# An edge stage of gathers and masked sums against one of dense products over counted edges, in a graph-attention and expert kernel on one core

## The reference, cut to what matters

```
x: 2500 nodes x 512;  src, dst: 40000 edges, sorted by dst
x = x + gnn(layernorm(x));   x = x + ffn(layernorm(x))

def gnn(nodes):
    h = nodes @ W + b_w                          # 2500 x 512
    s_dst, s_src = h @ a[:512], h @ a[512:]
    e = leaky_relu(s_dst[dst] + s_src[src] + b_a, 0.2)
    w = exp(e)
    alpha = w / segment_sum(w, dst)[dst]
    return segment_sum(alpha[:, None] * h[src], dst)

def ffn(x):   # 8 experts 512 -> 256 -> 512, the best 2 of a node, weighted by the softmax
```

## Time and profile before

| what | us |
|---|---|
| median of 3 runs (770.01, 776.66, 770.19) | 770.19 |
| the profiled execution, from its first to its last instruction | 843.5 |
| of that, up to the first gather | 85.5 |
| from there to the reciprocal of the denominators | 486.2 |
| from there to the end | 271.8 |

### The profile page before, as it was taken

One profiled execution on the slowest core, in us unless ns is written; L12 is line 12 of the kernel. 1 busy time (PEld: TensorE's weight loads), 2 busy tenths in 40 slices (PEclk: granted clock), 3 DMA queues, 4 the chain that ended last, 5 costly groups with the idle time before them and its releaser, 6 DMA issues.

```text
span 843.5 us, 13398 instructions
## 1 busy us (share of the span) xinstructions
PE 630.6 (75%) x2874; PEld 497.9 (59%) x2875; DVE 456.8 (54%) x1139; ACT 356.8 (42%) x956; POOL 478.4 (57%) x550
## 2 busy tenths in 40 slices
PE   4997335766676757766686667774988899999992
PEld 2886224655564646655565555662645787888881
DVE  3999224564555546645555655579758433333331
ACT  3232323343443434433443434335864444545551
POOL 4461775666665666656666566501104377777773
PEclk9999677989999998798979889995998999999997
DMA  9482675656666656666666666505897277777765
GB/s 310 154 286 103 179 211 146 194 166 178 186 177 174 187 168 189 175 183 167 185 184 182 169 179 189 164 2 188 306 352 285 66 136 133 137 135 134 138 117 71
DMA packets 59260, 147.26 MB, mean 175 GB/s; under 512 B 8965, under 2 KB 18437, under 8 KB 58968
## 3 DMA queue, kind: packets, MB, share of 16 engines
q0 software_dynamic: 35216, 106.84, 50.3%
q1 hardware_dynamic: 24008, 40.01, 13.7%
HBM read 118.46 MB, written 28.35 MB: 174 GB/s over the span
## 4 chain that ended last, share of the span: by engine, by line
PE 45%; DVE 21%; issue 14%; DVEq 7%; another core or an unknown queue 6%; DMA 3%; SPq 1%; ACT 1%; POOLq 0%; POOL 0%; ACTq 0%
PE ps L686 22%; PE ps L825 8%; PE ps L839 6%; DVE acc L1171 4%; DVE S L1162 4%; DVE Wt L1150 3%; DVE junk L1096 3%; PE ps L736 2%; PE ps L815 2%; DVE rows L1089 1%; DMA x_all<-in_x_dram 1%; DVEq L1202 1%; DVEq L1171 1%; PE ps L727 1%
## 5 line engine op out<-in xcount | busy, mean ns | idle before, releaser
L686 PE MATMUL ps<-rows,S 128*128 128x257 f32 x1252 | 325.9, 423 | 156.9 <-DVE acc L1171 107.1
L508 POOL DMA_INDIRECT rows<-node_table,srcT x313 | 298.4, 953 | 178.5 <-issue 86.7
L686 PEld LDWEIGHTS ps<-rows,S 128*128 128x128 f32 x1252 | 263.1, 214 | 219.5 <-issue 160.7
L915 ACT ACTIVATE E<-sdst_w,rows 128x128 f32 x313 | 100.1, 390 | 284.0 <-DVE Wt L1150 187.7
L1171 DVE TENSOR_TENSOR acc<-acc,ps 64x514 f32 x160 | 110.1, 688 | 147.8 <-PE ps L686 68.6
L1162 DVE SCALAR_TENSOR_TENSOR S<-ps,lane,Wt 128x128 f32<-128x128 f32 x313 | 88.2, 345 | 26.3 <-issue 13.9
L915 ACT ACTIVATE ps<-sdst_w,rows 128x128 f32 x313 | 96.0, 350 | 0.0
L825 PE MATMUL ps<-W_e,xgT 128*128 x352 | 83.4, 380 | 0.0
L604 POOL DMA_INDIRECT out_dram<-y,si x44 | 70.4, 1601 | 12.1 <-issue 6.3
L825 PEld LDWEIGHTS ps<-W_e,xgT 128*128 128x128 f32 x352 | 63.4, 190 | 6.9
L645 PE MATMUL ps<-Wb,xT 128*128 128x512 f32 x240 | 56.5, 398 | 6.0 <-DVE Wb L1108 5.0
(11 more groups left out here) (202 smaller groups left out, 612.9 us busy)
## 6 DMA issues: line engine op xcount, KB each, us to landing
W_e<-in_L_ffn_W_dram SPq DMA_DIRECT2D x16, 512.0 KB, 8.9
node_table<-rows SPq DMA_DIRECT2D x20, 258.0 KB, 3.2
xf<-in_x_cols_dram SPq DMA_DIRECT2D x10, 512.0 KB, 6.1
out_dram<-acc SPq DMA_DIRECT2D x20, 256.0 KB, 2.6
xn_table<-xn SPq DMA_DIRECT2D x20, 256.0 KB, 2.4
rows<-node_table,srcT POOLq DMA_INDIRECT x313
x_all<-in_x_dram SPq DMA_DIRECT2D x19, 256.0 KB, 6.6
b_b<-in_L_ffn_b_dram SPq DMA_DIRECT2D x1, 2048.0 KB, 14.6
```

Of the source, the lines that this page charges most:

```text
L508: nc.gpsimd.indirect_dma_start(out=rows[:, g % RING, c, :], out_offset=None, in_=table, in_offset=bass.IndirectOffsetOnAxis(ap=srcT[:, GC ...
L686: m = pe.matmul(ps_agg[q][:, a, 0:HALF], S[:, w, c, :], rows[:, r, c, a * HALF:(a + 1) * HALF], start=(c == 0), stop=(c == n - 1))
L915: m = nc.scalar.activation(e[:, c, :], sdst_w[:, bass.ds(w, 1), :].rearrange("p w n -> p (w n)"), ACT.Exp, bias=bias, scale=scale)
```

## The change: what it does

The edge stage is replaced; the node stage is altered, and the expert stage loses the sum of x and acc/denominator.

The nodes are laid out anew, 125 to a tile. h is kept in SBUF as an fp32r part `H_hi` (a copy by ACT from `hrow`) and a rest `H_lo` (a subtraction by POOL); `node_table`, its stores, the gathers and the ring go. An edge is the pair (lo, key): lo is src modulo 125, key is dst * 20 + src // 125. A tile of 125 targets has 2500 keys, five PSUM banks of 500, ten halves of 250. For each half three chunks of 128 edges are compared (with these inputs no half needs a fourth, so the branches for extras are not taken): DVE writes two bf16 one-hots for a chunk, 250 and 128 wide (`hot`), 60 instructions a tile, and PE multiplies them, 30 matmuls of 250 columns, so that a bank holds the counts. ACT makes the dense weights of a tile, exp(relu(0.8 s) + 0.2 s), with 40 instructions of 125 columns for two tiles ahead (`weights_of`). DVE multiplies weights and counts bank by bank, reading the bank in the order k, n where it is stored n, k (`weigh`), sums them over k (`sums_and_low`), and forms the rest `A_lo` beside ACT's fp32r copy `A_hi`. PE then forms 60 products of 512 columns a tile: A_lo H_hi, A_hi H_hi, A_hi H_lo. The counts of the next tile stand behind every fourth of the first 20 products and every fourth of the next 20; the last 20 have none. `add_x` divides and adds x.

```diff
+            def tile_products(t, s):                                  # PE
...
+                for k in range(NT):
+                    if k % (NT // 4) == 0:
+                        pe.wait_ge(A_lo_ok, 4 * t + k // (NT // 4) + 1)
+                    m = pe.matmul(ps_agg[s][0:TN, :], A_lo[:, k, :], H_hi[:, k, :], start=(k == 0), stop=False)
...
+                    if k % 4 == 3 and counts:
+                        count(t + 1, k // 4)
+                for k in range(NT):
+                    for H in (H_hi, H_lo.bitcast(F32R)):
+                        m = pe.matmul(ps_agg[s][0:TN, :], A_hi[:, s, k, :], H[:, k, :], start=False,
...
+                    if k < NT // 2 and k % 2 == 1 and counts:
+                        count(t + 1, NT // 4 + k // 2)
+                    if k == NT // 2 - 1 and counts:
+                        count_extras(t + 1)
...
+            def hot(key, low, chunk, half):                           # DVE
+
+                nc.vector.tensor_scalar(key, lane_k[:, :], offset[:, bass.ds(half, 1)],
+                                        keyT[:, bass.ds(chunk, 1)], ALU.add, ALU.is_equal)
+                return nc.vector.tensor_scalar(low, lane_l[:, :], loT[:, bass.ds(chunk, 1)], None,
+                                               ALU.is_equal)
+
+            def pairs_of(t):
+
+                words_of(dve, regs, t)
+                for h in range(HALVES):
+                    first_chunk = dve.snap(within(dve.snap(regs[h]), 0, CH - 1))
+                    if not (isinstance(t, int) and t == 0 and h < SLOTS):
+                        dve.wait_ge(count_ok, HALVES * t + h + 1 - SLOTS)
+                    for c in range(BASE - h % 2):
+                        m = hot(hot_k[:, h % SLOTS, c, :], hot_l[:, h % SLOTS, c, :], first_chunk + c, t * HALVES + h)
...
+            def weigh(t, s):
+
+                dve.wait_ge(exp_ok, t + 1)
+                for b in range(BANKS):
+                    dve.wait_ge(bank_ok, BANKS * t + b + 1)
+                    part = weight[:, s, :, b * BN:(b + 1) * BN]
+                    nc.vector.scalar_tensor_tensor(out=part, in0=part, scalar=FINITE,
+                                                   in1=ps_count[b][:, 0:BC].rearrange("p (n k) -> p k n", k=NT),
+                                                   op0=ALU.min, op1=ALU.mult).then_inc(A_ok, 1)
+
+            def sums_and_low(t, s):
+
+                dve.wait_ge(A_ok, BANKS * t + BANKS)
...
+                nc.vector.tensor_reduce(weight_sum[:, s, :], weight[:, s, :, :].rearrange("p k n -> p n k"), AX.X, ALU.add)\
+                    .then_inc(sum_ok, 1)
...
+                for q in range(4):
+                    some = slice(q * NT // 4, (q + 1) * NT // 4)
+                    dve.wait_ge(A_hi_ok, 4 * t + q + 1)
+                    nc.vector.tensor_tensor(A_lo[:, some, :], weight[:, s, some, :], A_hi[:, s, some, :].bitcast(F32),
+                                            ALU.subtract).then_inc(A_lo_ok, 1)
...
+            def tile_step(t, s):
+                peeled = isinstance(t, int)
+                more = not (peeled and t >= NT - 1)
+                if more:
+                    pairs_of(t + 1)
+                if not (peeled and t < 1):
+                    add_x(t - 1, 1 - s)
+                if more:
+                    weigh(t + 1, 1 - s)
+                    sums_and_low(t + 1, 1 - s)
...
+            def weights_of(t, s, high):                               # ACT; 20 Relu, then 20 Exp, 125 columns each
...
+                for k in range(NT):
+                    if k % (NT // 2) == 0:
+                        act.wait_ge(relu_ok, 2 * t + k // (NT // 2) + 1)
+                    m = nc.scalar.activation(weight[:, s, k, :], weight[:, s, k, :], ACT.Exp, bias=ss[:, 1, k:k + 1])
+                    if k == NT // 2 - 1 and high is not None:
+                        high_weights(*high)
```

More of the change, by code:

```diff
@@ L894, in step @@
                     std_of(u + 2, s)
-                if not (isinstance(u, int) and u < 1):
-                    scores(u - 1, 1 - s, i)
+                if u >= 1:
+                    high_rows(u - 1, 1 - s)
+                    scores(u - 1, 1 - s)
             for u in range(NT // 2):
@@ L936, in _ @@
-            act.wait_ge(odd_ok, 2)
-            act.wait_ge(win_ok, 2)
-            act.wait_ge(cst_ok, 1)
-            nc.scalar.activation(spare[:, 2:3], cst2[:, 0:1], ACT.Exp)
-            with act.Fori(0, NG // RING) as i:
-                window_words(act, regs, i)
-                for r in range(RING):
-                    group(r, i)
-            window_words(act, regs, NG // RING)
-            for r in range(NG % RING):
-                group(r, NG // RING, GC if r < NG % RING - 1 else GC_LAST)
+                n = min(4, NT - 4 * b) * TN
@@ L1122, in step @@
+            def step(u, s, ahead):
                 rstd_of(u, s)
@@ L1268, in _ @@
+            dve.wait_ge(H_lo_ok, NT)
+            over_node_tiles(dve, tile_step)
+            add_x(NT - 1, 1)
+            dve.wait_ge(x1_ok, NT)
             nc.vector.memset(spare[:, 0:1], 0.0).then_inc(acc_ok, 1)
             def x1_of(u, s):
-                for j in range(2):
-                    a = features(2 * u + j)
-                    nc.vector.scalar_tensor_tensor(out=a, in0=a, scalar=rden[:, bass.ds(2 * u + j, 1)],
-                                                   in1=halves(x_of(2 * u + j)), op0=ALU.mult, op1=ALU.add).then_inc(x1_ok, 1)
```

751 lines of the change are left out of this document (381 added, 370 removed).

## The result

The changed kernel takes 951.7 us (median of 4 runs, 950.0 to 952.6), the kernel before 770.1 in the same session. The ratio is 1.234, 95% interval 1.229 to 1.239. I had forecast 851 and a range up to 910: the sign was right and the loss more than twice as large, 181 us instead of 81. The profiled execution has a span of 950.9 us, as its run. The profile therefore stretches the changed kernel by nothing that can be seen, and the 73 us between profile and runs before went with what the change took out. That agrees with my placing them in the edge stage's gathers; no run separates the gathers from the rest of that stage.

What follows compares the result with a forecast made beforehand. Gathers were taken to set the old edge stage's pace. 122.3 + 446.5 (19 periods) + 16.7 = 585.5 against 571.7 before; span 843.5 + 13.8 - 1.4 = 856, less 5 is 851 us, range 775 to 910.

Steps and rivals of the forecast that it cites:

- What the gathers cost in the profile: Edge stage before: nearly all of the profile's 73.3 us over the median run lies in gathers; 5 taken for remaining stages.
- Node stage and ends: Before and behind the edge loop: last dot product at 96.4, tile 0 starts at 122.3, last tile ends 16.7 on.
- The period: Edge loop, one tile: 14.3 us on PE, then 9.2 of weigh, sum, first low piece and signals; 23.5 together.
- cold clock 1.7: Edge loop, PE after its wait for `A_lo`: half of 3.4 us at the lower clock level, 1.7 added a tile.
- the queue starts 1.6 early: Edge loop, DVE: its queue begins the one-hots during long instructions, so 12.1 us a tile count as 10.5.
- The sum's stride: DVE's sum over k: reading 2500 elements 500 bytes apart makes it 5.0 us, against 2.75 if the stride were free.
- the rival without strides: DVE's sum over k takes 2.75 us, period 21.2, time 806 us; chance 0.20.
- The stride in PSUM: DVE's `weigh`: reading its bank 80 bytes apart costs nothing, 0.65 us an instruction, 3.3 for five.
- The one-hots: DVE, edge loop: registers in the queue set their pace, 0.32 us a pair and 0.25 a half, 12.1 a tile.
- One-hots at full rate: Rival, DVE: one-hots miss the fast rate, 0.53 us a pair, 16 a tile, period 28.5, 946 us; chance 0.06.
- PE sets the pace: Rival, edge loop: last 20 products hide the stretch from last count to first low piece; 17.2 a tile, 730 us; chance 0.13.
- signs that I had named for being wrong: Changed profile: PE's wait under 1 us, the sum at 2.8, or a span far above the changed kernel's runs.

Runs made afterwards that it cites:

- Experiment 1: Changed kernel; in the node stage ScalarE rounds the rows of step u-1 before, not after, copying the features of step u+2: 909.9 us.
- experiment 2: As Experiment 1, and GpSimd's low rows lag the feature subtraction by two steps instead of one: 908.0 us.
- experiment 9: Changed kernel, only the ten groups of counts moved, behind products 12, 15, ... 39 instead of 4, 8, ... 40: 929.6 us.
- (6): Changed kernel with 14 filler products on TensorE before each tile's own: 938.4 us.
- experiment 5: Changed kernel with the one-hots of some halves made in other forms (constants, fixed addresses, fewer elements), counts mostly wrong: 952.1 us, one run.

## Why the prediction was wrong

**What the gathers cost in the profile: right as far as the runs show.** Span and run agree now to 1.7 us. That the gathers set the pace of the edge stage before was argued from the earlier trace rows and tested by no run; the forecast does not need it.

**Node stage and ends: wrong, +48.7 us.** The failed step is "POOL's two subtractions a step ... and ACT's two copies ... both fit beside DVE's 6". I added up durations per engine (5.2 and 1.2 beside 6) and never asked in which order the two in-order engines issue them. Each was indeed idle for more than half of the time (ACT busy 61 us, POOL 51, of 171). But the change placed a rounding behind a copy that waits for the products, and a subtraction behind the rounding's consumer, so that the copy, root, rounding, `H_lo` and subtraction became a loop with the products. Experiment 1 took 39.2 us off the start by swapping two calls, experiment 2 another 2.2. Of the remaining 7.3 us (129.6 against 122.3) 4.5 lie ahead of the end of DVE's last dot product, which I had at 96.4 and which comes at 100.9 in experiment 2, and the rest behind it. One part of them is visible below as small instructions held up by GpSimd; they were not split further.

**The period: wrong, +2.7 us, +50 in all.** The failed step is the stretch from the first low piece to the next weighing, 14.3 us on PE's side ("40 products with all 30 counts ... 12.4", cold clock 1.7, signal 0.2) and 13.9 on DVE's ("so it is just not late"). It took 17.5, and both sides were too short.

DVE's side is 16.2. I had 10.5 for the one-hots, because "the queue starts 1.6 early"; the engine needs 12.6 for them, and it begins them behind the low pieces. With that side alone the period would be 8.75 + 16.2 = 25.0, which is what experiment 9 measured.

PE's side is longer still. I compared two totals, PE's and DVE's, and took the larger. They are not side by side: the counts stand in PE's order between the products, the first behind 4 of them, so PE stops until the first pairs are there. These waits are 32.4 us over 19 tiles, 1.7 a tile, for which the sum had nothing. And PE works 6.5 us a tile at the lower clock level, not 3.4, which costs 3.3 and not 1.7. Together 12.4 + 0.2 + 1.7 + 3.3 = 17.6.

So of the 2.7 us a period 1.5 are DVE's own work and 1.2 PE's lateness. The second share is measured: giving PE work ahead of its first wait gives back 22.1 us, 1.2 in each of 19 periods (9). Fillers that warm the clock give 13.2 (6), and faster one-hots give nothing as long as PE is late (5).

**The sum's stride: right in size.** 4.97 against 5.0; taking it away was worth 21 us and not 42, since it had covered most of the load of words at the loop's end. "Hidden under the sum" was right inside the loop's body; over its end 0.6 to 0.8 us show even in the changed kernel. I drew nothing from the sentence for the rival without strides, whose 806 us was too low for that reason as well.

**The stride in PSUM: right, free.** 0.670 in the mean, and 3.0 us for five where I had 3.3.

**The one-hots: near in sum by luck, wrong in reason.** 12.6 us a tile against 12.1. I named the queue, 0.32 a pair and 0.25 a half; it is the engine, 0.257 + 0.161, of which 0.18 fetches operands. The head start of 1.6 us came from the same wrong reason. And the edit that follows is not static addresses but one operand fewer.

**The rivals.** None happened. The 946 us of "One-hots at full rate" is near the measured time by luck: it has 16 us of one-hots a tile and a period of 28.5, and they took 12.6 and 26.2. "PE sets the pace" was nearest in its mechanism, and on the wrong side: I had PE as a bound only where it is full. Here PE bounded the stage while idle 0.20 of it, because its work was unlocked late and ran slowly. None of the signs that I had named for being wrong appeared either: PE waits 3.5 us a tile for `A_lo` (53.1 over 15) and not under 1, the sum takes 5.0, and the span agrees with the run. They tested the terms that I doubted and not the two that failed.

## What to carry to other kernels

For engines that issue in order, adding up durations gives a floor, not a time: for each instruction that waits, write down what stands behind it on its queue and who waits for that, round the loop, before calling it hidden. If two engines hand work to each other in small pieces, put enough independent work ahead of the first hand-over to cover it, and keep enough for the stretch behind the last; check which one bounds by making the busier one faster, as experiment 5 did. Before moving work to an idle GpSimd ask what VectorE does in that time.

## What the hardware showed that I had not expected

VectorE and GpSimd took turns by whole instructions in the node stage too. Timeline of the kernel of experiment 2, a product of 4 elements beside GpSimd's `H_lo`:

```profile
76.22 1.30 POOL L504 TENSOR_TENSOR H_lo<-hrow,H_hi 128x512 fp32r<-128x512 f32 x1 [0.47 <-ACT H_hi L922]
...
76.72 0.81 DVE L1137 TENSOR_TENSOR s_dot<-s_raw,rstd 128x4 f32<-128x4 f32 x1
```

Both end at 77.5. In the changed kernel such products took 0.90 us in the mean, where the one with no GpSimd instruction beside it took 0.16, and one instruction on 20 elements of one partition 2.32, beside a feature subtraction of GpSimd of 2.34:

```profile
L1135 DVE TENSOR_TENSOR s_dot<-s_raw,rstd 128x4 f32<-128x4 f32 x10 | 9.0, 900 | 0.3
...
L1213 DVE TENSOR_SCALAR ex_t<-ex_t 1x20 f32<-1x20 f32 x1 | 2.3, 2324 | 0.0
```

The Trainium skill, SBUF — State Buffer, section "Who interferes with whom", names both kinds: an instruction with two inputs from SBUF, and a `tensor_scalar` in a fast mode. The trace agrees. The reduction over the weights ran beside no GpSimd work, so nothing here shows how it would fare.

An operand fetched per partition costs a VectorE instruction 0.061 us, as much as 235 bf16 elements. The load of eleven words took 1.3 or 2.5 us, longer than the 0.81 for six, and around the end of a loop VectorE's queue went on 3.1 us later than inside the body. What of that is the branch and what the code behind it was not tried.

Fourteen filler products a tile, 3.2 us of work that nothing needs, made the kernel 13 us faster, by holding the granted clock at 1.00 for the first products.
